# A graph network on one core: in the message pass, sums loaded ahead of masks, stores issued by SyncE, the cap moved to GpSimd, the shift given to the exponential as its bias, and rows copied by ScalarE and the vector engine by turns

## The reference

```python
total = jnp.concatenate([atom_fea[dst], atom_fea[src], edge_fea], axis=1)
total = _batchnorm(total @ fc_w.T + fc_b, bn1_w, bn1_b)
gate, core = jnp.split(total, 2, axis=1)
messages = jax.nn.sigmoid(gate) * jax.nn.softplus(core)
aggr = jax.ops.segment_sum(messages, dst, num_segments=N)
```

## Time and profile before

| | |
|---|---|
| median of three runs | 11063.14 us |
| profiled execution | 11011.23 us, span 11009.5 us |
| message pass, first GpSimd instruction to last store landed | 5724.8 to 6537.9 us |
| busy share of the span | PE 59%, DVE 52%, ACT 29%, POOL 63% |
| steps of the message pass | 196 |

### The profile page before, as it was taken

How to read it: one execution, slowest core, us unless ns; L and a number is a source line. 1 busy time by engine, 2 the same in 40 slices (tenths; PEclk the granted TensorE clock), 3 DMA queues, 4 the chain that set the end, 5 groups by cost and what they waited for, 6 DMA issues and landing times. The chain is left out here.

```text
span 11009.5 us, 139032 instructions
## 1 busy us (share of the span) xinstructions
PE 6475.1 (59%) x43115; PEld 5514.4 (50%) x43115; DVE 5772.1 (52%) x8056; ACT 3166.4 (29%) x4896; POOL 6970.1 (63%) x6971
## 2 busy tenths in 40 slices
PE   4776666558888666666654433554555455555553
PEld 3555555457788544554432213554545445545543
DVE  3555555689941555555558865333333433333335
ACT  1333333237700111111127751222222222222221
POOL 4777777716400577777764454777777657777774
PEclk9888888769989788888875556777777767777776
DMA  7666666514446477777755542344444334444442
GB/s 129 193 191 197 189 194 193 156 75 195 184 186 274 150 238 239 234 235 236 239 194 193 191 146 71 122 126 126 124 126 122 93 99 125 123 126 124 126 125 69
DMA packets 1298130, 1783.26 MB, mean 162 GB/s; under 512 B 618169, under 2 KB 793068, under 8 KB 1288346
## 3 DMA queue, kind: packets, MB, share of 16 engines
q1 hardware_dynamic: 815543, 882.53, 24.8%
q10 hardware_dynamic: 269696, 616.64, 15.2%
q0 software_dynamic: 212704, 281.43, 10.6%
HBM read 921.96 MB, written 857.87 MB: 162 GB/s over the span
## 5 line engine op out<-in xcount | busy, mean ns | idle before, releaser
L603 POOL DMA_INDIRECT arena<-table_d,idx_src x3136 | 2959.2, 944 | 1176.2 <-issue 955.1
L747 PE MATMUL pn<-work,wblk 128*128 128x128 f32 x3136 | 957.8, 404 | 1891.9 <-DMA arena<-table_d,idx_src 1891.9
L603 POOL DMA_INDIRECT arena<-in_x_dram,idx_src x1568 | 1520.2, 969 | 583.7 <-issue 476.9
L603 POOL DMA_INDIRECT arena<-tsrc_d,idx_src x1568 | 1479.8, 944 | 477.9 <-issue 477.9
L1277 DVE TENSOR_SCALAR idx_src<-src_all 128x8 int32 (+1 forms) x784 | 139.6, 179 | 3109.9 <-PE pn L748 2381.8
L747 PEld LDWEIGHTS pn<-work,wblk 128*128 128x128 f32 x3136 | 754.4, 296 | 1967.3 <-DMA arena<-table_d,idx_src 999.4
L748 PE MATMUL pn<-ident,arena 128*128 128x128 f32 x4704 | 1294.7, 372 | 0.0
L1036 ACT ACTIVATE arena<-pn 128x512 f32<-128x512 f32 x1470 | 792.4, 594 | 1266.6 <-PE pn L779 1192.3
L748 PEld LDWEIGHTS pn<-ident,arena 128*128 128x128 f32 x4704 | 1096.9, 287 | 0.0
L737 PE MATMUL pn<-work,weT 128*128 128x512 f32 x784 | 551.7, 793 | 665.2 <-DMA arena<-tsrc_d,idx_src 636.1
L1322 DVE TENSOR_TENSOR_SCAN work<-keep,work,pn 128x512 f32<-128x512 bf16 x588 | 752.9, 1280 | 270.9 <-PE ph L760 201.4
(11 more groups left out here) (347 smaller groups left out, 13718.9 us busy)
## 6 DMA issues: line engine op xcount, KB each, us to landing
runs_d<-arena ACTq DMA_DIRECT2D x588, 768.0 KB
adj_d<-feat SPq DMA_DIRECT2D x37, 3136.0 KB, 10.7
feat<-adj_d SPq DMA_DIRECT2D x37, 3136.0 KB, 10.6
seed_d<-nothing SPq DMA_DIRECT2D x392, 256.0 KB
arena<-seed_d SPq DMA_DIRECT2D x392, 256.0 KB, 6.8
attr<-in_edge_attr_dram SPq DMA_DIRECT2D x392, 256.0 KB
feat<-total_d SPq DMA_DIRECT2D x196, 512.0 KB
keep<-keep_d SPq DMA_DIRECT2D x588, 128.0 KB
```

The lines of the kernel that those rows point to most:

```text
L603: g.indirect_dma_start(out=to, out_offset=None, in_=table, in_offset=bass.IndirectOffsetOnAxis(ap=idx, axis=0))\
L747: mm(to, wblk[:, PNA.index(p), j, :], feat_to[u], start=True, stop=False, skip_group_check=True)
```

## The change

In the message pass SyncE now issues the sums of two blocks together and ahead of the masks; it also issues the stores, which ScalarE did before. In a loop turn it stores block 0 of the turn before after the first pair of sums, and blocks 1, 2 and 3 of the turn before after the second pair. GpSimd computes three halves: the scaled and capped argument of the exponential, without the shift, for both halves (the cap is `room` = 80 minus the shift), and for the core half the scaled and shifted value as before. ScalarE adds the shift as the bias of the exponential, which is therefore two instructions of 512 columns instead of one of 1024. The vector engine's cap is gone. The turned rows go to two PSUM banks by turns; blocks 0 and 2 are copied by ScalarE, blocks 1 and 3 by the vector engine. Here is the diff with little of its context:

```diff
@@ -187,7 +187,7 @@
         agg2 = sb("agg2", [P, 2])
-        bnsc, bnbi = sb("bnsc", [P, 2]), sb("bnbi", [P, 2])
+        bnsc, bnbi, room = sb("bnsc", [P, 2]), sb("bnbi", [P, 2]), sb("room", [P, 2])
         nrow = sb("nrow", [P, 4, F])
@@ -230,7 +230,7 @@
         s_eC = ring("s_eC", one((STAT, *PNA)))
-        s_col = ring("s_col", {**one(GATHER), MSG: 2})
+        s_col = ring("s_col", {**one(GATHER), MSG: 3})
         s_zero_out = sem("s_zero_out")
@@ -238,7 +238,7 @@
         s_top = ring("s_top", one((SOFT, MSG)))
-        s_arg = ring("s_arg", one((SOFT, MSG)))
+        s_arg = ring("s_arg", one((SOFT,)))
         s_dec = ring("s_dec", one((SOFT, MSG)))
@@ -447,6 +447,14 @@
+            def gated_store(i, u):
+
+                s_rev.done(sp, MSG, i, u)
+                sp.sem_inc(s_in_order, 1)
+                sp.dma_start(runs1_d.rearrange("(h n) c -> h n c", h=2)[:, bass.ds(blk(i, u) * BLK, BLK), :]
+                             .rearrange("h (p j) c -> p h (j c)", j=J),
+                             obuf_f[:, u * BLK:(u + 1) * BLK].rearrange("p (h q) -> p h q", h=2)).then_inc(s_out.sems[u], 16)
+
             def adjacency_moves(p):
@@ -512,8 +520,12 @@
                             if p == MSG:
-                                attr_load(p, i, u)
-                                mask_load(p, i, u)
+                                if u % 2 == 0:
+                                    attr_load(p, i, u)
+                                    attr_load(p, i, u + 1)
+                                    mask_load(p, i, u)
+                                for v in ((0,), (), (1, 2, 3), ())[u]:
+                                    gated_store(i - 1, v)
                             elif p == SOFT:
@@ -531,6 +543,9 @@
+                if p == MSG:
+                    for u in range(U):
+                        gated_store(IT - 1, u)
                 if p in READS:
@@ -609,8 +624,10 @@
                 for part in range(2):
-                    g.tensor_scalar(zbuf[:, u, part * BLK:(part + 1) * BLK], totals[:, u, part * BLK:(part + 1) * BLK],
-                                    bnsc[:, part:part + 1], bnbi[:, part:part + 1], ALU.mult, ALU.add).then_inc(s_col.sems[u], 1)
+                    g.tensor_scalar(ebuf[:, u, part * BLK:(part + 1) * BLK], totals[:, u, part * BLK:(part + 1) * BLK],
+                                    bnsc[:, part:part + 1], room[:, part:part + 1], ALU.mult, ALU.min).then_inc(s_col.sems[u], 1)
+                g.tensor_scalar(zbuf[:, u, BLK:], totals[:, u, BLK:], bnsc[:, 1:2], bnbi[:, 1:2], ALU.mult, ALU.add)\
+                 .then_inc(s_col.sems[u], 1)
@@ -772,11 +789,11 @@
                     return
-                s_rev.done(pe, p, i, u, back=1)
+                s_rev.done(pe, p, i, u, back=2 if p == MSG else 1)
                 for k in range(UNITS[p]):
                     for j in range(J):
-                        last = nc.tensor.transpose(pt[:, k, j * P:(j + 1) * P], of[:, 1 + j:1 + BLK:J], ident[:, :])
+                        last = nc.tensor.transpose(pt[:, u % 2 if p == MSG else k, j * P:(j + 1) * P], of[:, 1 + j:1 + BLK:J], ident[:, :])
                 last.then_inc(s_row.sems[u], 1)
@@ -1023,12 +1040,19 @@
+            def gated_rows(i, u):
+
+                s_row.done(act, MSG, i, u)
+                s_out.done(act, MSG, i, u, back=U)
+                A(obuf_f[:, u * BLK:(u + 1) * BLK].rearrange("p (h j c) -> p j h c", h=2, j=J),
+                  pt[:, u % 2, :].rearrange("p (j h c) -> p j h c", j=J, h=2), ACT.Copy).then_inc(s_rev.sems[u], 1)
+
             def rows_out(p, i, u):
                 K = UNITS[p]
-                to = rows_to[u] if K == 3 else obuf_f[:, u * BLK:(u + 1) * BLK]
+                to = rows_to[u]
                 for k in range(K):
@@ -1038,8 +1062,7 @@
                 s_rev.done(act, p, i, u)
-                r = runs3_d if K == 3 else runs1_d
-                act.dma_start(r.rearrange("(h n) c -> h n c", h=2)[:, bass.ds(blk(i, u) * BLK, BLK), :]
+                act.dma_start(runs3_d.rearrange("(h n) c -> h n c", h=2)[:, bass.ds(blk(i, u) * BLK, BLK), :]
                               .rearrange("h (p j) c -> p h (j c)", j=J),
@@ -1055,8 +1078,9 @@
-                s_arg.done(act, MSG, i, u)
-                A(ebuf[:, u, :], ebuf[:, u, :], ACT.Exp).then_inc(s_exp.sems[u], 1)
+                s_col.done(act, MSG, i, u)
+                A(ebuf[:, u, 0:BLK], ebuf[:, u, 0:BLK], ACT.Exp, bias=bnbi[:, 0:1])
+                A(ebuf[:, u, BLK:], ebuf[:, u, BLK:], ACT.Exp, bias=bnbi[:, 1:2]).then_inc(s_exp.sems[u], 1)
                 s_exp.done(act, MSG, i, u)
@@ -1100,10 +1124,8 @@
                             logs(*nx2)
-                        if u > 0:
-                            rows_out(p, i, u - 1)
-                        elif not (isinstance(i, int) and i == 0):
-                            rows_out(p, i - 1, U - 1)
+                        if u % 2:
+                            gated_rows(i, u - 1)
                         continue
@@ -1201,8 +1223,6 @@
                 body(p, IT - 1, True)
-                if p == MSG:
-                    rows_out(p, IT - 1, U - 1)
                 if p == SOFT:
@@ -1327,10 +1347,12 @@
-            def capped(i, u):
-
-                s_col.done(dve, MSG, i, u)
-                TS(ebuf[:, u, :], zbuf[:, u, :], CAP, None, ALU.min).then_inc(s_arg.sems[u], 1)
+            def gated_rows(i, u):
+
+                s_row.done(dve, MSG, i, u)
+                s_out.done(dve, MSG, i, u, back=U)
+                V.tensor_copy(obuf_f[:, u * BLK:(u + 1) * BLK].rearrange("p (h j c) -> p j h c", h=2, j=J),
+                              pt[:, u % 2, :].rearrange("p (j h c) -> p j h c", j=J, h=2)).then_inc(s_rev.sems[u], 1)
@@ -1431,8 +1453,10 @@
                         softplus(i + (u + 1) // U, (u + 1) % U)
-                    if not (end and u + 2 >= U):
-                        capped(i + (u + 2) // U, (u + 2) % U)
+                    if u == 2:
+                        gated_rows(i, 1)
+                    if u == 0 and not (isinstance(i, int) and i == 0):
+                        gated_rows(i - 1, U - 1)
                     s_cus.done(dve, p, i, u)
@@ -1443,8 +1467,6 @@
                 if p == MSG:
-                    capped(0, 0)
-                    capped(0, 1)
                     softplus(0, 0)
@@ -1458,6 +1480,8 @@
                     step(p, IT - 1, u, True)
+                if p == MSG:
+                    gated_rows(IT - 1, U - 1)
@@ -1805,6 +1829,7 @@
             link(TS(bnbi[:, 0:1], bnbi[:, 0:1], -1.0, None, ALU.mult))
+            link(TS(room[:, :], bnbi[:, :], -1.0, CAP, ALU.mult, ALU.add))
             dve.sem_inc(s_wc, 1)
```

## The result

The changed kernel takes 11354.49 us (median of four runs, 11348.52 to 11370.23) beside 11067.95 us before (four runs): a ratio of 1.0263, with a 95% interval of 1.0248 to 1.0278. It is slower by 286 us where 133 us less were forecast. The profiled execution has a span of 11350.9 us.

What follows compares the result with a forecast made beforehand. It took the message pass to be bound by a chain of waits, 16.58 us per four steps. The new chain's terms summed to 13.8 us, over 48 turns 133 us less: 10930 us, range 10865 to 11005.

Steps and rivals of the forecast that it cites:

- The bound before: Message pass before: a closed chain scan, masks, sums, GpSimd, cap, logs, softplus, 16.58 us per four steps, no engine at its limit.
- Term 3: GpSimd's share of the new chain: three instructions instead of two, 949 ns each, 2.85 us, the minimum costed at nothing.
- Rival A: Message pass: loads hidden and the vector engine bounds at 3.2 us a step, 184 us less, 10879 us; chance 0.19.
- Rival B: Message pass: GpSimd and vector engine block each other, GpSimd bounds at 3.67 us a step, 92 us less, 10971; chance 0.15.
- Rival C: SyncE's one queue: sums wait for up to three stores, 17.7 us a turn, 55 us more, 11118 us; chance 0.05.
- The chain: New message-pass loop of row copy, store, sums, GpSimd, ScalarE, vector engine: 13.8 us a turn, 3.45 a step; chance 0.57.
- The bias: ScalarE's exponential: a column operand adds some 93 ns each, making term 4 some 0.2 us longer and the turn 14.0 us.
- Copies: Row copies by turns: the vector engine's takes 0.69 us; ScalarE's earlier 0.71 us a step behind copy and store is dropped.

Runs made afterwards that it cites:

- e4: Kernel before with only SyncE's order of loads changed, two sums ahead of the masks: 13379.69 us against 13446.17, ratio 0.9956.
- e1: Kernel before with test GpSimd instructions, four of each form, put ahead of everything: multiply and minimum took 2063 ns, multiply and add 765.
- e9: Changed kernel with GpSimd's minimum replaced by an addition of zero, cap left out: 10946.45 us against 11051.49 for the kernel before, ratio 0.9908.
- e5: Kernel before with only the cap moved to GpSimd as multiply and minimum, exponential with bias: 11298.78 us against 11048.85, ratio 1.0235.
- e10: e9 with the store of block 3 moved behind the next turn's first pair of sums: 10911.6 us, ratio 0.9877 to the kernel before.
- e6: Changed kernel with cap back on the vector engine, single exponential, all row copies by ScalarE: 11072.85 us against 11048.85 for the kernel before, ratio 1.0027.
- e11: e6 with the store of block 3 moved behind the next turn's first sums: 10944.85 us against 11051.49 for the kernel before, ratio 0.9905.
- e2: Same kernel as e9, run on the slower chip: 13326.88 us against 13446.17 for the kernel before, ratio 0.9914.

## Why the prediction was wrong

**The bound before: right.** The period of 4.14 us, the chain from scan to masks to sums, and that no engine was at its limit: e4 cuts that chain with nothing else, and the period falls by 0.37 us.

**Term 3, GpSimd: the step that failed.** I wrote that the capped ones end in a minimum instead of a sum, and costed that at nothing, "as shape and operands are of the same kind". No row of the trace before shows a minimum on GpSimd. An operation that the trace doesn't show needs a bound from both sides, and I took one point in its place, so that neither the range nor any rival held the outcome. Three instructions came to 5.64 us a step and not 2.85; that alone put GpSimd above every chain. e1 shows the price of the operation with the vector engine idle (2063 against 765 ns), e9 that without it the time falls into the stated range (105 us less), e5 that this part alone costs 250 of the 286 us.

**Rival A: out of reach.** e10 cuts the chain, and the step is 3.56 us where A had 3.2; GpSimd's work and waits fill it, not the vector engine's 3.14 us.

**Rival B named the right engine for a wrong reason.** It has GpSimd bound at 3.67 us by a fight for the way to SBUF. What the engines took from each other is real but small: L627 took 2576 ns at most against 2065 at least, 0.51 us. Nor did one shut the other out for a whole instruction: in the changed kernel a softplus ran from 6206.94 to 6207.79 inside an L627 that took its 2.07 us. In e9, with nothing slow, the mean is 0.95 and not 1.2. That e9's step of 3.65 us is near B's 3.67 is chance: GpSimd waited for sums for 135 of 560 us there.

**Rival C: a mechanism that exists and didn't act.** In the changed kernel GpSimd had no wait for sums, so SyncE was never late. In e6 it acted, in the form that not the queue but SyncE's own order holds the sums, and it cost 0.7 us a step.

**The chain: right in kind, 0.9 us a turn short.** Between its loads at 6101.89 and 6116.60 e9 has 14.7 us where I had 13.8. By terms: from load to GpSimd 4.26 (3.8 forecast), three instructions 2.27 (2.85), to the softplus 2.48 (2.3), softplus, scan, product, softplus and copy 4.54 (4.2), from the copy's end to the load 1.16 (0.63). The errors partly cancel; the last is the worst in proportion, as between the copy's end at 6115.44 and the loads at 6116.60 SyncE issues a store as well, done at 6116.06, and I had counted no time for it. Forecast for this kernel without the minimum: 133 us less; measured with e9: 105. And the chain was hardly above the next bound: cutting it gave e10 only 0.09 us a step.

**The bias.** The exponential of 512 columns took 706 to 722 ns against the 630 of one without a column: 76 to 92 ns more. That is close to the 93 ns that the Trainium skill gives for a column operand (ScalarE: Activation LUTs, What ACT_TABLE_LOAD costs), and the trace agrees with it.

**Copies: right.** 677 ns for the vector engine's, forecast 0.69; 579 for ScalarE's. ScalarE's wait of 0.71 us a step behind its store is gone.

## What to carry to other kernels

When work moves to an engine, price the operation and not its shape: an ALU operation that the trace doesn't show on that engine has no price until it is measured, and its range must be wide enough to make the engine the bound. Measure it first with four instructions at the start of a kernel; that settled here in one run what no reading of the trace could. And where one engine issues both loads and stores in order, a store whose data comes late must not stand ahead of a load that the others wait for: e6 and e11 differ by that one place, and by 128 us.

## What the runs showed of the hardware

- GpSimd's tensor_scalar on 128x512 f32 has a quick form and slow ones, here with columns as operands: multiply-add 765 ns, multiply-multiply 770 (multiply-add with immediates 618); with minimum, maximum or subtract second, or minimum first, 2063 to 2074; a single multiply, minimum or maximum 1558 to 1564. A product or sum of two tensors takes 1261.
- So on GpSimd a multiply and an add is half the price of a multiply alone, 765 ns against 1564; with an add of zero the pair took 767 in e9, the median of 305.
- In the changed kernel a product of the vector engine, 0.69 us long, that runs at the start of a GpSimd instruction lengthens that one by about 0.51 us (at 6203.16 L629 took 1.29 us and not 0.77). A softplus that came in the middle of a GpSimd instruction didn't lengthen it and took 0.85 us itself (at 6206.94).
- The same kernel took 11051 us on one chip and 13446 on another, TensorE's granted clock being 0.77 and 0.69; the ratios of the same variant (e2 and e9) agree within their intervals, 0.9914 and 0.9908.
